# Grouped attention on one Trainium2 core: the order of VectorE's work inside a step, and which of its instructions frees the output bank

## The reference

```python
h = norm_scale * x / (norm(x) * d ** -0.5 + 1e-8) * split_scale
q = h @ Wq.T        # 8 heads of 64
k = h @ Wk.T        # 2 groups of 64
v = h @ Wv.T        # 2 groups of 64
attn = softmax(q @ k.T / 8)          # 512 x 512 per batch and head
out = x + (attn @ v) @ Wo.T          # x: the normalised input
```

## Time and profile before

| | |
|---|---|
| median of 3 runs | 1576.61 us (1574.97 to 1576.76) |
| the profiled execution | 1577.04 us |
| its span in the trace | 1575.1 us |
| third stage in the trace | about 330 to 990 us |
| period of a middle batch of it | 80.13 us |

### The profile page before, as it was taken

How to read it: one execution, slowest core, us unless ns; L and a number is a source line. 1 busy time by engine, 2 the same in 40 slices (tenths; PEclk the granted TensorE clock), 3 DMA queues, 4 the chain that set the end, 5 groups by cost and what they waited for, 6 DMA issues and landing times.

```text
span 1575.1 us, 21341 instructions
## 1 busy us (share of the span) xinstructions
PE 1455.0 (92%) x7252; PEld 1189.2 (76%) x7252; DVE 1020.4 (65%) x2048; ACT 821.7 (52%) x1571; POOL 725.1 (46%) x963
## 2 busy tenths in 40 slices
PE   5999999879999999999999997599899999999996
PEld 4888788757787878787878775477688888888884
DVE  6888789677888788888888876445333423424233
ACT  4666557468878787878787763321221213212221
POOL 4788546543455554545454445122334333243332
PEclk9999999989999999999999999799999999999998
DMA  7555023220002020202020201332010010110100
GB/s 204 138 153 135 21 94 107 96 92 1 1 1 81 1 81 1 81 1 81 1 81 1 101 1 54 94 100 67 2 54 33 21 53 0 54 53 0 53 27 27
DMA packets 46205, 88.51 MB, mean 56 GB/s; under 512 B 2720, under 2 KB 3744, under 8 KB 46112
## 3 DMA queue, kind: packets, MB, share of 16 engines
q1 hardware_dynamic: 42416, 79.98, 14.9%
q0 software_dynamic: 3696, 7.34, 2.9%
HBM read 62.14 MB, written 25.17 MB: 55 GB/s over the span
## 4 chain that ended last, share of the span: by engine, by line
PE 74%; DVE 13%; POOL 4%; issue 4%; ACT 3%; DMA 2%; SPq 0%; POOLq 0%; DVEq 0%
PE f_inner L57 23%; PE context L1618 13%; PE f_down L2044 9%; PE context L57 7%; PE score L57 5%; PE turned L1653 5%; PE score L854 3%; DVE g_ptl L1542 2%; PE context L1681 2%; PE context L1679 2%; DVE g_neg_max L1528 2%; PE turned L57 1%; DVE f_wl L1968 1%; PE f_inner L2016 1%; POOL g_prob L1246 1%
## 5 line engine op out<-in xcount | busy, mean ns | idle before, releaser
L1246 POOL TENSOR_SCALAR g_prob<-g_prob,g_inv_sum 128x512 f32<-128x512 f32 x256 | 177.9, 695 | 308.7 <-DVE g_inv_sum L1533 308.6
L57 PE MATMUL f_inner<-f_xth,f_wh 128*128 128x512 f32 x704 | 281.3, 400 | 15.6 <-DVE f_wl L1968 12.7
L57 PE MATMUL f_inner<-f_xtl,f_wh 128*128 128x512 f32 x704 | 279.6, 397 | 0.0
L1878 ACT ACTIVATE f_silu<-f_inner,f_inner_scale 128x512 f32<-128x512 f32 x88 | 60.8, 691 | 413.9 <-PE f_inner L57 413.9
L1937 DVE SCALAR_TENSOR_TENSOR f_hidden<-f_inner,f_inner_scale,f_silu 128x512 f32<-128x512 f32 x88 | 66.0, 750 | 313.8 <-PE f_inner L57 313.8
L1826 POOL TENSOR_TENSOR f_hl<-f_hidden,f_hh 128x512 fp32r<-128x512 f32 x88 | 127.9, 1454 | 297.1 <-DVE f_hh L1943 297.1
L1528 DVE TENSOR_REDUCE g_neg_max<-score 128x1 f32<-128x512 f32 x256 | 175.4, 685 | 83.5 <-PE score L57 82.3
L1360 ACT ACTIVATE g_prob<-score,g_neg_max 128x512 f32<-128x512 f32 x256 | 177.3, 693 | 99.4 <-DVE g_neg_max L1528 97.3
L1542 DVE TENSOR_TENSOR g_ptl<-turned,g_pth 128x512 fp32r<-128x512 f32 x256 | 173.9, 679 | 15.2 <-ACT g_pth L1408 13.4
L1653 PE MATMUL turned<-identity,g_prob 128*128 128x128 f32 x1024 | 155.9, 275 | 25.9 <-DVE g_ptl L1542 25.9
L57 PEld LDWEIGHTS f_inner<-f_xth,f_wh 128*128 128x128 f32 x704 | 133.3, 189 | 54.3 <-DVE f_wl L1968 17.3
(11 more groups left out here) (231 smaller groups left out, 3401.3 us busy)
## 6 DMA issues: line engine op xcount, KB each, us to landing
xt<-x_t SPq DMA_DIRECT2D x16, 512.0 KB, 5.8
x_mixed<-x_resident SPq DMA_DIRECT2D x8, 1024.0 KB, 4.3
x_pair<-x_mixed SPq DMA_DIRECT2D x8, 1024.0 KB, 8.0
g_res<-x_mixed SPq DMA_DIRECT2D x8, 1024.0 KB, 6.5
x_attended<-g_res SPq DMA_DIRECT2D x8, 1024.0 KB, 5.2
x_pair<-x_attended SPq DMA_DIRECT2D x8, 1024.0 KB, 5.6
x_resident<-x SPq DMA_DIRECT2D x7, 1024.0 KB, 12.6
factor_sum<-factors POOLq DMA_DIRECT2D x7, 1024.0 KB, 10.6
```

What stands on the lines that cost most here:

```text
L57: last = nc.tensor.matmul(out, lhsT, rhs, start=(n == 0), stop=(n == len(pairs) - 1))
L1246: nc.gpsimd.tensor_scalar(prob[:, at, :], prob[:, at, :], inv_sum[:, at:at + 1], 1.0, ALU.mult, ALU.mult).then_inc(prob_ready, 1)
```

## The change

Three things are changed in `grouped_attention`, all in VectorE's program. The low part of a side piece (q, h, k, v) moves from step END+2, ahead of `g_ptl`, to step END+1, behind `g_ptl`. With that `g_ptl` is no longer behind a side low part. In `total_of` the addition that reads the side bank signals `side_free` itself, and `bn_stats` signals `total_ready`; the waits in between and before the aggregation follow. No instruction is added or taken away.

```diff
@@ total_of
                 nc.vector.tensor_tensor(total[:, t, :], side[side_at(f"wo{t}")][:, :], xn[:, t % 2, :],
-                                        ALU.add).then_inc(total_ready, 1)
-                dve.wait_ge(total_ready, b * T + t + 1 + 2)
-                nc.vector.bn_stats(obn[:, t, :], total[:, t, :]).then_inc(side_free, 1)
+                                        ALU.add).then_inc(side_free, 1)
+                dve.wait_ge(side_free, use + 1)
+                nc.vector.bn_stats(obn[:, t, :], total[:, t, :]).then_inc(total_ready, 1)
                 if t == T - 1:
-                    wait_alone(dve, s, side_free, use + 1)
+                    dve.wait_ge(total_ready, (b + 1) * T + 2)
@@ step
                     nc.vector.reciprocal(inv_sum[:, at:at + 1], row_sum[:, at:at + 1]).then_inc(inv_ready, 1)
-                for name in side_done(u, first, last, drain, 2):
-                    if name in SPLIT:
-                        lo_of(b, p, name)
                 turn_u = u - TURN_LAG
...
                                             pth[:, at, :, cols].bitcast(F32), ALU.subtract).then_inc(lo_ready, 1)
                 for name in side_done(u, first, last, drain, 1):
-                    if name not in SPLIT:
+                    if name in SPLIT:
+                        lo_of(b, p, name)
+                    else:
                         total_of(b - 1, side_use(b, name), int(name[2]))
```

## The result

The changed kernel takes 1588.97 us, the median of 4 runs (1587.58 to 1589.98). The kernel before took 1576.68 beside it (4 runs, 1574.97 to 1576.80). The ratio is 1.0078, with a 95% interval of 1.0066 to 1.0091: 12.3 us, or 0.78%, slower. The profiled execution has a span of 1587.9 us; before it was 1575.1.

A forecast was written before the change was run, and what follows sets the result against it. PE was taken as the bound, its early waits set by DVE's reciprocal through POOL and ACT. Six middle batches +8.6, first +0.8, last -0.7: +8.7 us, so 1585.3 us, range 1580 to 1590.

The forecast's parts named there:

- The bound: Middle batch: 76.84 of 80.13 us PE-busy; steps 8 to 10 wait on a chain from DVE's reciprocal through POOL and ACT.
- the five waits: PE's idle 3.29 us per middle batch, placed before steps 8, 9, 10, 15 and 32, all ended by DVE.
- A: Steps 2 and 3: q1's low part delays the reciprocal and POOL's `normalise`; +1.5 us a batch, bounds 1.1 and 1.6.
- B: q2, q3, h0, h1 moved ahead of the next maxima and reciprocal: exponentials have time; nothing, 0 to 0.2 us a batch.
- C: Steps 24 to 32: q0's new place wins 0.6 us, k's delay of ACT eats it; 0, bounds -0.6 and +0.2.
- D: h3's wait of 0.49 us goes but mostly returns at step 17; gain 0.06 us a batch, bounds 0.06 and 0.49.
- E: First and last batch: first +0.8 us, bounds -0.5 and +1.6; last -0.7, bounds -1.4 and 0.
- the signs named for the profile: Included a middle-batch period of 81.4 to 81.7 us and a step 32 wait within 0.2 of 1.28.
- R1: Faster: q3's place in DVE's queue holds step 9, q0's place wins 0.6 in seven batches; -6.0 us, about 1570.6; chance 0.09.
- R2: No difference: q1's delay only partly paid, under 0.5 us a batch; total -1 to +3, about 1577.5; chance 0.11.
- R3: Much slower: q1's delay paid in full, k's delay lengthens the step 32 wait by 0.6; +15.4 us, 1592; chance 0.08.
- R4: The bank is freed sooner but nothing comes of it; alone it moves 2 us at most; no separate chance given.

The follow-up runs named there:

- experiment 2: The kernel before with only q1's low part moved, to step 2 behind `g_ptl` and ahead of the statistics: 1589.24 us.
- experiment 1: The changed kernel with only q1's low part put back into step 3: 1585.82 us.
- experiment 5: The changed kernel with q1's and q2's low parts both put back in their old places: 1578.48 us, ratio 1.0007.
- 9: The kernel before with only q2's low part moved, to step 4 behind `g_ptl`: 1581.12 us.
- 7: The kernel before with the first half of POOL's scales issued ahead of `normalise` in step 3: 1576.20 us, ratio 0.9997.
- experiment 3: The changed kernel with q1's low part still in step 2, but behind the statistics and their aggregation: 1588.79 us.
- 12: The changed kernel with q2 and k put back, POOL's scales ahead of `normalise`, and q1 in step 2 behind the statistics: 1572.52 us, ratio 0.9980.
- 8: The changed kernel with q1, q2 and k put back and POOL's scales ahead of `normalise` in step 3: 1573.14 us, ratio 0.9977.
- 6: The changed kernel with only k's low part put back into step 25: 1588.88 us.
- 4: The kernel before with only the bank freed by the addition: 1576.87 us, ratio 1.0002.
- 11: The changed kernel with q1, q2 and k put back and POOL's order as before: 1572.88 us, ratio 0.9979.
- 10: The kernel before with only k's low part moved, to step 24: 1579.81 us.

## Why the prediction was right, point by point

The forecast was slower by 8.7 us, 1585.3 us, in a range of 1580 to 1590. Measured were 12.3 us and 1588.97. Direction, place and mechanism of the main term hold; the size is 3.6 us short in the medians. Three terms were missing or mis-sized besides, and part of the agreement is luck: of the six middle batches, 1.5 us that nobody counted were won at step 18, and 1.6 us more than forecast were lost at step 32.

**The bound.** Held. The delay, 1.79 us at step 9, arises before it, in the chain from the reciprocal through POOL and ACT. The statement that it is POOL's chain and not q3's low part is shown by experiment 2, in which q3 is not moved. The statement was incomplete in two points. There was a second chain through the exponentials of step 5, 0.13 us behind POOL's (experiments 1, 5 and 9), and a third through the `normalise` of step 4, 0.07 us behind (7). And the five waits were not all: the stall of wo2 at step 17 was in the 76.84 us that the prediction took as busy, of which it said that nothing else could shrink.

**A, q1.** The mechanism was right, link by link, and experiments 2, 3 and 12 show it. Its size was 1.8 and not 1.5, above the upper bound of 1.6. The 1.39 of the pair are there. The rest is small: step 2's maxima came 0.14 later for what stands ahead of them, the pair starts 0.70 us after the start of `g_ptl` where the statistics before started 0.59 after it, and the maxima of step 3 follow the aggregation by 0.41 instead of 0.29. The pair's own cast is not the reason (it had ended at 574.73, 0.18 before the pair starts). The bound had taken "a backlog of about 0.15" as the worst and nothing for such gaps. Experiment 2 alone gives 1.70, so some 0.1 comes from the rest of the change. Against the 1.5 taken, the 1.79 at step 9 make 1.7 us in six batches.

**B, the other low parts.** Right in the sum and wrong in its reason. It said that the exponentials behind the moved maxima have time. For q2 they don't: it costs 0.59 us a batch alone. It cost nothing here only because q1's delay is longer and covers it. Alone the two cost 1.70 and 0.59, together (81.95 against 80.28) 1.67: the larger one counts, not the sum. q3, h0 and h1 cost 0.13 us at step 9 at most (experiment 5). And h2, which B does not name, wins: its low part a step earlier frees wo2's bank, 0.24 us a batch.

**C, k and q0.** Both parts are real, the balance was not 0. In the changed kernel, from step 24 of the same batch on (k's cast, then DVE and ACT up to step 0 of the next), the timeline shows:

```profile
632.51 1.39 DVE L1465 TENSOR_TENSOR g_kl<-context,g_kh 64x512 fp32r<-64x512 f32 x2 [1.12 <-ACT g_kh L1342]
633.93 0.43 DVE L1500 CAST g_oh<-g_out_sum 128x512 fp32r<-128x512 f32 x1
634.39 0.69 DVE L1528 TENSOR_REDUCE g_neg_max<-score 128x1 f32<-128x512 f32 x1
635.12 0.69 ACT L1360 ACTIVATE g_prob<-score,g_neg_max 128x512 f32<-128x512 f32 x1 [0.66 <-DVE g_neg_max L1528]
...
645.69 1.39 DVE L1461 TENSOR_TENSOR g_q<-context,g_q 64x512 fp32r<-64x512 f32 x2 [0.15 <-ACT g_q L1338]
...
647.91 0.67 DVE L1539 TENSOR_TENSOR g_ptl<-turned,g_pth 128x512 fp32r<-128x512 f32 x1
```

DVE stands 1.12 us for k's cast, with `g_oh` and the maxima of step 25 queued behind. The exponentials of step 25 come at +68.34; before, +66.05. Less the 1.53 by which PE's step 24 is late already, that is 0.76 later (0.6 was forecast). Tile 26 comes at +81.13 against +79.30, 0.30 later after the same 1.53, where the prediction had worked out 0.08 and taken 0, with 0.2 as its upper bound; PE's step 32 is 0.27 later than its step 31. q0's new place wins 0.47 and not 0.6 (8), k takes 0.74 and not 0.6 (6). In six batches this is 1.6 us over the forecast. It did not show in the total because h2's place won 1.5 at step 18.

**D, the bank.** Held: the delay is 0.07 us smaller at step 17 than at step 9 (1.72 against 1.79), and alone it gives nothing (4).

**E.** Forecast +0.8 and -0.7, measured +1.1 and -0.7. The second agreement is luck. In the last batch the wait of 2.04 is 1.58 now, which is 0.46. The rest can't be told from the clock: summed over windows of 1 us, the last batch of before had 17.2 us at the low clock and that of the change 14.0, and experiment 3, whose last batch has the same order as the change's, took 107.2 us with 8.4 at the low clock, 1.1 less than the change. The first batch had 4.2 and 3.2 us at the low clock.

**The clock, a term that was missing.** The prediction took the clock as constant, since it was 1.00 in every middle batch of before. Two of six batches fell to 0.98 and paid 1.00 and 0.64 us. This makes 1.6 us; windows and a timeline of PE show it below. In the profiled executions the loss is 12.8 us of span, 4.1 over the forecast: 1.7 from A, 1.6 from C less the 1.5 of h2, some 0.4 from D (0.03 us a batch at the score of step 17 instead of 0.06) and drifts of hundredths, 1.6 from the clock, 0.35 from E, less the 0.15 of the rest, make 4.0. For the same reasons two of the signs named for the profile were missed: the period is 81.95, outside 81.4 to 81.7, and the wait at step 32 moved by 0.21, just over 0.2.

**The rivals.** R1, that q3's place holds step 9, falls: `normalise` and `g_h` moved with the reciprocal, and q1 alone costs everything. Its second half, that q0's place wins if nothing eats it, is true in kind (0.47, not 0.6) and makes experiments 8, 11 and 12 faster, together with h2. R2 falls: the delay was paid in full. R3 was nearest in time (1592) and right in part: k's delay did go beyond C's balance, by 0.27 us a batch and not by 0.6. R4 holds for the bank alone.

## What to carry to other kernels

An instruction that is moved up in an in-order queue is paid for by the one that it pushes back: follow that one (here a reciprocal of 0.15 us) through every queue to the engine that sets the time, and look at whether the moved one's own operand is there yet. Ask then for the second chain that ends at the same place: with two that tie within 0.13 us, undoing one delay gave back a quarter (experiment 1), speeding up one gave nothing (7, where a third chain stood 0.07 us behind), and two delays on them cost the larger, not the sum. Busy time can hide a stall: the one of wo2 was to be seen in the weight loads and not in the matmuls. A change of many places can hold two that win (q0, 0.47 us a batch, and h2, 0.24) and three that hide them: taken one by one, they turned 0.78% slower into 0.2% faster.

## What was not expected of the hardware

The granted clock fell, from the upper of its two levels (2.4 GHz) to the lower (1.2 GHz), inside batches in which PE was busy for 95% of the time (78.55 of 82.95 us). The changed kernel, windows of 3 us in the first middle batch, from +22.76 on, then the same stretch of the batch at 566.78, whose clock stayed:

```profile
424.00:427.00 3.00, 2.05 (x10) 1.77 (x11) 2.48 (x6) 2.33 (x6) 0.69 (x1) 0.77 0.00 0
427.00:430.00 3.00, 3.00 (x13) 2.32 (x12) 3.00 (x8) 2.65 (x7) 2.63 (x3) 0.66 0.00 0
...
589.54:592.54 3.00, 2.06 (x13) 1.71 (x14) 2.48 (x6) 2.32 (x6) 0.69 (x1) 1.00 0.00 0
592.54:595.54 3.00, 2.59 (x14) 1.92 (x13) 3.00 (x8) 2.66 (x7) 2.63 (x3) 1.00 0.00 0
```

PE's timeline of the first of these:

```profile
425.58 1.08 PE L1652 MATMUL turned<-identity,g_prob 128*128 128x128 f32 x4 [0.71 <-DVE g_ptl L1539]
426.31 0.78 PE L57 MATMUL score<-g_kh,g_q 128*128 128x512 f32 x1
427.31 0.63 PE L1678 MATMUL context<-g_pth,g_v 128*128 128x512 f32 x1
...
429.69 0.39 PE L57 MATMUL score<-g_kl,g_q 128*128 128x512 f32 x1
```

The clock fell at 425.6, right behind the stalls of steps 8 and 9, none of them over 0.71 us, and was back at 429.0 (windows of 0.5 us show 0.60 from 425.5, 0.50 up to 429.0 and 0.99 from there): 1.08 us for the four transposes where it is 0.63, and 0.63 for a matmul of 512 columns where it is 0.39. The waits were the same in the batch in which it stayed. A batch with such a fall was 0.3 to 1.4 us longer than one of the same kernel at full clock (one of experiment 3, at 0.96, by 2.7). In the middle batches all falls were in kernels in which step 9 came 0.5 us or more late, by q1's or q2's new place (the change, 1, 2, 3, 6 and 9: 17 of 36 batches); the kernel before and the seven others, 4, 5, 7, 8, 10, 11 and 12, had none in 48. In 1 and 6 a shorter batch came with more falls than in the change: against six batches at full clock these took 4.2 and 4.7 us, in the change 1.7.

The first and the last batch are different, and there the clock fell in the kernel before too. This is its last batch, behind the wait of 2.04 us at 903.81:

```profile
904.00:907.00 3.00, 3.00 (x13) 2.38 (x12) 2.96 (x8) 1.52 (x4) 1.40 (x2) 0.63 0.00 0
```

In the first batch of 1, 5 and 8 the clock fell 24 to 28 us behind the score of step 2; their first batches took 67.8, 68.0 and 68.2 us, that of 11, without such a fall, 66.2. So a late step 9 goes with the falls in the middle batches and is not the only thing that does. Idle PE on this chip can so cost more than its own length. What decides in which of such batches the clock falls was not tried and stays open.
